# Graph attention block: who copies the split parts, who makes the target masks, and where one guard product stands

## The reference

```
h   = relu(layernorm(x))
msg = h_neigh[None] + E[adj]             # the edge type is adj itself; only adj == 1 is attended to
q   = h @ Wq.T + bq                      # 512 targets x 8 heads x 16
k,v = msg @ Wk.T + bk, msg @ Wv.T + bv
scores = einsum(q, k) / 4                # masked where adj == 0
attn = softmax(scores), 0 where adj == 0
out  = x + (attn . v) @ Wo.T + bo
```

## Time and profile before

| | |
|---|---|
| median of 3 runs | 52.49 us |
| the profiled execution | 52.74 us |
| its span, first to last instruction | 50.6 us |
| busy in the span | TensorE 44.1 us (87%), VectorE 40.3 (80%), ScalarE 34.7 (68%), GpSimd 31.0 (61%) |
| granted TensorE clock | 0.99 of full speed over the span |
| chain that ended last, by engine | TensorE 62%, VectorE 15%, DMA 8%, ScalarE 5% |

### The profile page before, as it was taken

The page is one execution under the profiler, slowest core; times in us unless marked ns, Lnnn a source line. Parts: engine busy times, 40 slices in busy tenths (PEclk is TensorE's granted clock), DMA queues, the critical chain, the costliest instruction groups (busy, mean ns, idle before and its releaser), DMA issues.

```text
span 50.6 us, 844 instructions
## 1 busy us (share of the span) xinstructions
PE 44.1 (87%) x257; PEld 17.8 (35%) x260; DVE 40.3 (80%) x115; ACT 34.7 (68%) x60; POOL 31.0 (61%) x50
## 2 busy tenths in 40 slices
PE   0899879978999679899999999999999998999800
PEld 0333215824445233234344424142222023288500
DVE  2011879598489999799999999799997999989820
ACT  0380657789996978979999898897199999400000
POOL 5790001999999999547599959990999930000000
PEclk9999999999999999999999999999999999999996
DMA  0689999960099999700000000000000000000032
GB/s 0 76 219 431 435 379 235 403 269 2 10 212 193 184 295 201 154 2 0 0 0 0 0 6 0 13 0 0 0 0 0 0 0 0 13 0 0 0 118 89
DMA packets 2070, 4.98 MB, mean 98 GB/s; under 512 B 258, under 2 KB 658, under 8 KB 1810
## 3 DMA queue, kind: packets, MB, share of 16 engines
q1 hardware_dynamic: 1490, 2.44, 21.2%
q10 hardware_dynamic: 576, 2.49, 12.7%
HBM read 3.08 MB, written 0.26 MB: 66 GB/s over the span
## 4 chain that ended last, share of the span: by engine, by line
PE 62%; DVE 15%; DMA 8%; ACT 5%; issue 3%; DVEq 0%
PE ps L609 15%; PE ps L577 11%; DMA xt<-x_dram 8%; PE ps L623 8%; PE ps L563 7%; PE ps L633 6%; PE ps L586 4%; PE ps L604 3%; PE ps L547 2%; PE ps L512 2%; DVE ctxT L476 2%; DVE stats L368 2%; DVE split L396 2%; DVE y L489 2%; DVE turned_U L467 2%
## 5 line engine op out<-in xcount | busy, mean ns | idle before, releaser
L426 DVE CUSTOM_DVE_ANT_0 masked_scores<-ps,mask_b 128x512 bf16<-128x512 f32 x32 | 20.1, 687 | 1.7 <-PE ps L563 1.0
L233 POOL TENSOR_TENSOR prob<-prob,live 128x512 int32<-128x512 int32 x10 | 12.6, 1275 | 0.0
L351 ACT ACTIVATE prob<-ps 128x512 f32<-128x512 f32 x21 | 11.4, 598 | 1.1 <-PE ps L609 0.8
L609 PE MATMUL ps<-stack 98*128 98x512 bf16 x32 | 10.9, 381 | 0.6 <-ACT stack L323 0.4
L577 PE MATMUL ps<-stack 96*128 96x512 bf16 x28 | 9.6, 384 | 0.2
L215 POOL TENSOR_SCALAR mask_b<-adj_b_sb 128x512 bf16<-128x512 int32 x3 | 6.3, 2111 | 4.8 <-DMA adj_b_sb<-adj_b_dram 4.8
L351 ACT ACTIVATE prob<-masked_n 128x512 f32<-128x512 f32 x11 | 6.4, 626 | 1.5 <-DVE masked_n L446 1.4
L446 DVE TENSOR_TENSOR masked_n<-ps,veto 128x512 f32<-128x512 f32 x11 | 6.8, 683 | 0.4 <-PE ps L609 0.3
L503 PE MATMUL ps<-ones 128*128 128x512 bf16 x10 | 4.2, 604 | 1.4 <-DVE ones L361 1.4
L323 ACT ACTIVATE stack<-ps 2x512 bf16<-2x512 f32 x8 | 4.7, 590 | 0.4
L609 PEld LDWEIGHTS ps<-stack 98*128 98x128 bf16 x32 | 2.8, 97 | 6.0 <-DVE masked_n L446 2.2
(11 more groups left out here) (71 smaller groups left out, 54.8 us busy)
## 6 DMA issues: line engine op xcount, KB each, us to landing
stack<-split SPq DMA_DIRECT2D x8, 192.0 KB, 4.0
adj_b_sb<-adj_b_dram ACTq DMA_DIRECT2D x1, 1024.0 KB, 7.4
adj_n_sb<-adj_n_dram ACTq DMA_DIRECT2D x1, 1024.0 KB, 10.1
pk<-pack_k_dram ACTq DMA_DIRECT2D x1, 322.0 KB, 4.4
xt<-x_dram SPq DMA_DIRECT2D x1, 256.0 KB, 4.2
pw<-pack_w_dram SPq DMA_DIRECT2D x1, 256.0 KB, 6.0
out_dram<-y SPq DMA_DIRECT2D x1, 192.0 KB, 2.0
brow<-bias_rows_dram SPq DMA_DIRECT2D x1, 128.0 KB, 9.1
```

Source lines behind the costliest of these rows:

```text
L233: nc.gpsimd.tensor_tensor(bits, bits, live[:, LIVE_TILES.index(t), :], ALU.mult).then_inc(cut_done, 1)
L351: nc.scalar.activation(prob[:, h, t, :], scores, ACT.Exp, scale=DH ** -0.5).then_inc(exp_done, 1)
L426: nc.vector.tensor_tensor_reduce(out=masked_scores[:, k % len(A_BANKS), :], in0=ps[:, A_BANKS[k % len(A_BANKS)], :], in1=mask_b[:, t, :], ...
L609: nc.tensor.matmul(bank, stack[0:STACK, h, SIDE["k"], t * P:(t + 1) * P], stack[0:STACK, h, SIDE["q"], :], start=(h, t) not in ON_PE, stop ...
```

## The change

- GpSimd no longer makes masks. In their place it makes the four copies of parts, in the order k part 0, q part 0, k part 1, q part 1, and it sees a pair of bf16 values as one int32, so each row of 512 values is 256 elements.
- VectorE no longer copies. It makes all four target masks: tiles 0, 1 and 2 where the first three copies stood, tile 3 behind head 0's first maximum.
- The guard's product of the first accumulator moves behind head 1's third tile by target, ahead of the turning of head 0's maxima.

```
+            def copy_slots(name, n, ready):
+                home = HOME[name][n]
+                others = [s for s in range(SLOTS) if SLOT_PARTS[name][s] == n and s != home]
+                step = 3 if len(others) > 1 else 1
+                pairs = split[:, :, SIDE[name], :].bitcast(i32)
+                nc.gpsimd.tensor_copy(
+                    pairs[:, others[0]:others[-1] + 1:step, :],
+                    pairs[:, home:home + 1, :].to_broadcast([P, len(others), B // 2])).then_inc(ready, 1)
...
+            pool.wait_ge(k_part_ready, 1)
+            copy_slots("k", 0, k_copied)
+            for i in range(HALVES):
+                pool.wait_ge(q_part_ready[i], 1)
+            copy_slots("q", 0, q_copied)
+            pool.wait_ge(k_part_ready, 2)
+            copy_slots("k", 1, k_copied)
+            for i in range(HALVES):
+                pool.wait_ge(q_part_ready[i], 2)
+            copy_slots("q", 1, q_copied)
             make_live(3)
...
-                    if t in MASKS_ON_POOL:
-                        dve.wait_ge(mask_b_pool_ready, MASKS_ON_POOL.index(t) + 1)
-                    else:
-                        dve.wait_ge(mask_b_ready, 1)
+                    dve.wait_ge(mask_b_ready, t + 1)
...
             for t in range(BT):
-                if t == MASK_ON_DVE:
-                    make_mask_b(t)
                 find_max(0, t)
+                if t == 0:
+                    make_mask_b(BT - 1)
...
-            add_tiny(ACC_BANK, B)
             for t in range(BT):
                 score_head_0(t)
...
                 if k == 6:
+                    add_tiny(ACC_BANK, B)
                     turn_max(0)
```

More of the change, by code:

```diff
@@ L31 @@
 WARM_BANK = 5
-MASKS_ON_POOL, MASK_ON_DVE = (0, 1, 3), 2
 PIECES = ((0, 3), (3, BT - 3))
@@ L153, in gnn_kernel @@
         v_projected, v_ready, v_biased = sem("v_projected"), sem("v_ready"), sem("v_biased")
-        (mask_b_ready, mask_b_pool_ready, squares_ready, veto_even_ready, veto_odd_ready, veto_last_ready,
+        (mask_b_ready, squares_ready, veto_even_ready, veto_odd_ready, veto_last_ready,
          veto_bias_set) = (
-            sem("mask_b_ready"), sem("mask_b_pool_ready"), sem("squares_ready"), sem("veto_even_ready"),
+            sem("mask_b_ready"), sem("squares_ready"), sem("veto_even_ready"),
             sem("veto_odd_ready"), sem("veto_last_ready"), sem("veto_bias_set"))
@@ L380, in _ @@
                                         ALU.subtract, ALU.mult).then_inc(xn_ready, 1)
[L382 to L389, removed]
             def take_q_part(n):
@@ L397, in take_q_part, with make_mask_b @@
                                         ALU.add).then_inc(q_part_ready[1], 1)
+            def make_mask_b(t):
+                dve.wait_ge(adj_b_loaded, 16)
+                nc.vector.tensor_scalar(mask_b[:, t, :], adj_b_sb[:, t * N:(t + 1) * N], 0.0, MASKED,
+                                        ALU.is_equal, ALU.mult).then_inc(mask_b_ready, 1)
             dve.wait_ge(is_head_0_set, 1)
@@ L402, in _ @@
                                     ALU.mult).then_inc(k_head_0_ready, 1)
-            copy_slots("k", 0, k_copied)
+            make_mask_b(0)
             take_q_part(0)
@@ L406, in _ @@
                 q32_ready[1], 1)
-            dve.wait_ge(q_part_ready[0], 1)
-            dve.wait_ge(q_part_ready[1], 1)
-            copy_slots("q", 0, q_copied)
+            make_mask_b(1)
             take_q_part(1)
-            dve.wait_ge(q_part_ready[0], 2)
-            dve.wait_ge(q_part_ready[1], 2)
-            copy_slots("q", 1, q_copied)
+            make_mask_b(2)
             take_q_part(2)
-            dve.wait_ge(k_part_ready, 2)
-            copy_slots("k", 1, k_copied)
             def find_max(h, t):
@@ L429, in find_max @@
                     accum_out=row_max[:, h, t:t + 1]).then_inc(max_found, 1)
[L431 to L434, removed]
             adj_tiles = adj_n_sb[:, :].rearrange("p (t b) -> p t b", b=B)
```

## The result

The changed kernel takes 52.13 us, the median of 20 runs (51.77 to 52.80); the kernel before, run beside it, 52.53 us (20 runs, 52.04 to 52.98). The ratio is 0.9938, with a 95% interval of 0.9914 to 0.9963. Forecast were 52.14 us and faster. Runs more than 1.5% above the fastest of their kernel are left out of the ratios, so a ratio need not be that of the medians.

What follows compares the result with a forecast made beforehand. The start of the long stretch at 20.74 us, with TensorE and VectorE full, was taken to bound the kernel. Guard 0.31 plus VectorE 0.04 gave 0.35 us off the 52.49 median: 52.14 us, range 51.98 to 52.65.

Steps and rivals of the forecast that it cites:

- What bounds the kernel: From 20.74 to 35.76 us TensorE and VectorE are full; the edit can only move when this long stretch begins.
- The guard: On TensorE ahead of head 0's scores: without it the first product starts 0.31 us earlier, bounds 0.15 and 0.53.
- Its new place is free: After head 1's third tile, about 16.5 us, TensorE would wait for GpSimd's split maxima anyway, so the guard costs nothing.
- VectorE: Masks in place of copies: q's part 1 starts 0 to 0.15 us earlier; 0.04 taken.
- The rule weighed there: A VectorE copy or tensor-scalar in 2-port mode and a GpSimd instruction exclude each other; the trace agreed once, contradicted once.
- Rival 1: VectorE's second mask held by GpSimd's copy of price c; gain 0.26 at 0.75, slower from 1.0 us; chance 0.13 over 1.0.
- GpSimd's copies: Copies take 0.75 us for part 0, 0.43 for part 1; SyncE issues at 12.4, and head 1's data lands in time.
- Masks off GpSimd: GpSimd is free for `live` at about 12 instead of 14.88 us, so splitting head 0's maxima no longer waits for it.
- ScalarE's cap of 0.46: At V's reading, ScalarE was ready at 15.81 but started at 16.27, so only 0.46 us of TensorE's gain counts.
- The sum: Whole kernel: guard 0.31 plus VectorE 0.04 makes 0.35 us less.
- Rivals 2 and 3: 2: head 1's turning waits on GpSimd, no change, 52.45, chance 0.20. 3: late DMAs, 0.2 us slower, 52.7, chance 0.05.
- the copy of 11.60: VectorE's narrow copy took 0.29 us in the middle of GpSimd's mask of 10.80 to 13.02, contradicting the exclusion rule.

Runs made afterwards that it cites:

- the late third mask: Changed kernel with ScalarE's third neighbour-side mask (square and relu) moved behind exponential 20, VectorE waiting for it only at first use; ratio to before 0.9857, again 0.9884.
- that mask behind exponential 3: Changed kernel with the square of ScalarE's third neighbour-side mask behind the placing of head 0's maxima, its relu behind the fourth exponential; ratio to before 0.9959.
- the bf16 kernel: Changed kernel with GpSimd copying bf16 values one by one, 1024 and 512 elements a row instead of 512 and 256 int32; ratio to before 0.9970.
- three instructions fewer: Changed kernel with three memsets (neighbour-side mask's bias and the guard's row) on VectorE in place of GpSimd; ratio to before 0.9895.

## Why the prediction was right, point by point

**What bounds the kernel**: right for this change: the start of the long stretch moved by 0.54 and the end by 0.54, and with the late third mask both by 0.32 more. It is not the start alone: with that mask behind exponential 3 the start moved by 0.32 and the end by 0.05. (Ten maxima stand ahead of the awaited one on VectorE, not nine.)

**The guard**: right in place, too small in size. Forecast 0.31, bounds 0.15 and 0.53. From subtraction to first product 0.41 went, and the second pass comes another 0.11 sooner (11.93 - 11.50 = 0.43 us behind the first where it was 0.54): 0.52, near the upper bound. The sum took the guard's own slot, 0.31, on the premise that the product may start where the guard did. It starts 0.10 sooner, 0.12 us behind the subtraction where the guard stood 0.22 behind it, and its second pass gains the other 0.11. The lower bound was argued the wrong way round: the guard did not cover the product's weight load (it began at 12.08, with the product), while the subtraction covers it now. "Its new place is free" held in the changed kernel, where ScalarE came 0.5 us after the turning, and stopped holding when ScalarE was quicker.

**VectorE**: 0.04 forecast; q's part 1 ended at 11.33, 1.91 after the start of part 0, against 1.94 before: 0.03. The rule weighed there is borne out for copies: the second mask waited for GpSimd's copy (10.65 + 0.28) and in the bf16 kernel for the longer one. Rival 1's mechanism is thus real, only its price was low: c was 0.61, under the 0.75 that I took, and far from the 1.0 from which it decides; the bf16 kernel with c = 1.04 lost most of the gain. In both kernels the last subtraction came 0.07 later than the rival's formula says, counted as in the kernel before (11.53 against 11.46, and 11.96 against 11.89): the copy of q's part 0 started at 10.19 and not at 10.1, by the same count. The sum itself took 0.04 from VectorE at c = 0.75, where the rival's formula gives 0.05 the other way; that these two did not fit together had no consequence only because c was smaller.

**GpSimd's copies**: 0.61 and 0.46 to 0.59, against 0.75 and 0.43. Of the rows weighed, the memset was the nearest. SyncE's DMA at 12.35, which is 12.50 counted as in the kernel before, against 12.4; free as forecast.

**Masks off GpSimd**: its worth was named and not priced. Without it the turning waits for GpSimd and the guard's gain is 0.22 (0.04 to 0.24 over three profiles), not 0.54; the other way round the copies alone gain 0.03. The sum of parts was therefore right only for the whole change.

**ScalarE's cap of 0.46**: not quite right. V's reading came 0.54 earlier (15.58, while the mask before it ran to 15.66 by its record). Records of one engine overlap by 0.1 us, and the cap must be counted with that overlap: 0.54.

**The sum**: 0.35 forecast; 0.54 in the trace up to the last `y`, less about 0.15 at the end of the run that I had no step for, is 0.39; measured 0.40 between medians and 0.33 by the ratio (0.19 to 0.45). So the mechanism was right, but the closeness of the number is in part luck: two errors offset each other, the guard taken 0.2 too small and the longer end not seen.

**Rivals 2 and 3**: neither came. Head 1's turning started at 19.31 with its maxima split at 18.93, and the DMA was early.

## What to carry to other kernels

A term on TensorE ahead of a float32 product is to be read from start to start of its neighbours, over the next pass too, and not as the small product's own slot. Before summing the parts of a change, ask of each what the next-late engine would do without the others: here the guard was worth 0.22 alone, and less where GpSimd's masks took longer, and 0.51 on top of the copies. When a trace shows a gain up to the last result that the whole time doesn't, compare what follows the last result.

## What the runs showed of the hardware

**A list's length shows at the end.** GpSimd with 69 executed instructions took 0.41 to 0.44 us between its last two semaphore steps, with 66 instructions 0.08, whether copies or idle memsets made the difference. No other lengths were tried.

**VectorE waits for GpSimd's copies, and for its compares only near their end.** Masks of VectorE that came while GpSimd copied were held until 0.28 us after the copy's end (0.72 and 1.15 us for a mask of 0.42, the second from 0.87 us before the copy's end on). Against GpSimd's two-step compares of 1.92 to 2.22 us it depended on when VectorE came. In the changed kernel the fourth mask came at 13.29, 0.54 before the end of `live` at 13.83, and was held. In the kernel with the guard alone a wide copy at 10.23 took 0.41, undisturbed, 0.87 before the end of a GpSimd mask that ran from 8.88 for 2.22 us. Over all 14 profiles, every VectorE copy or mask that came 0.46 to 0.59 us before the end of a compare was held to 0.28 us after it (ten cases), and none that came 0.74 us or more before it was; one of those took 0.48 in place of 0.28, the others their plain time. So what the prediction took for a contradiction, the copy of 11.60, is a matter of when it came, 1.42 us before the compare's end. The Trainium skill (SBUF — State Buffer, Who interferes with whom) says that of GpSimd and a VectorE instruction in a 2-port mode the one that issues first holds the shared pair of ports for its whole instruction. For GpSimd's copies these traces agree; for its compares they agree only for VectorE instructions that came within 0.6 us of the end.

**The spread between runs begins in the first 7 us.** The first projection, two passes in TensorE's timeline, of the kernel before, the changed kernel, and the changed kernel again:

```profile
5.89 1.12 PE L506 MATMUL ps<-msgT,pk 128*128 128x512 f32 x2 [0.24 <-ACT msgT L282]
```

```profile
5.70 1.43 PE L502 MATMUL ps<-msgT,pk 128*128 128x512 f32 x2
```

```profile
5.69 1.97 PE L502 MATMUL ps<-msgT,pk 128*128 128x512 f32 x2
```

The warm-up products of 512 columns ahead of it start 0.43 us apart, which is the pace of 1.2 GHz (512 / 0.43 = 1.2 columns a ns), and in some runs the last ones 0.22, the pace of 2.4 GHz. TensorE had been busy without a pause from 1.44 us to the end of the warm-up in all of them. By this pace the step to the upper level came between 4.4 us and past 7 us, at different moments in different runs, though the granted clock is printed as 1.00 for that stretch each time. In the third row it came so late that q's part 0 was read 0.5 us later than in the second, and the whole run took 52.72 in place of 52.13 us, with the same 38.27 us behind it. The landing of `x` is the other source: it landed at 4.36 us in the profile with three instructions fewer and at 5.00 in that of copies and masks alone, and q's part 0 was read at 9.04 and 9.67. A measure that starts behind both repeated to 0.02 us where ratios of 12 runs had intervals of 0.6 to 0.9%.
